# Gate and up biases in a grouped MoE feed-forward kernel: a two-row matmul in each block's accumulation in place of a spread copy added by VectorE

## The reference

```python
logits = y @ router_weight                                # 16 experts
topk_w, topk_i = top_k(logits, 2); topk_w = softmax(topk_w)
gu   = einsum('th,ehf->tef', y, gate_up_proj) + gate_up_proj_bias   # 256 columns: gate, up, gate, up ...
gate = minimum(gu[..., ::2], 7);  up = clip(gu[..., 1::2], -7, 7)
act  = (up + 1) * gate * sigmoid(1.702 * gate)
out  = einsum('tei,eih,te->th', act, down_proj, scores) + scores @ down_proj_bias
return x + out
```

## Time and profile before

| | us |
|---|---|
| median of 3 runs | 187.59 |
| lowest and highest | 185.32, 188.4 |
| span of the profiled execution | 185.1 |

### The profile page before, as it was taken

One profiled execution on the slowest core, in us unless ns is written; L12 is line 12 of the kernel. 1 busy time (PEld: TensorE's weight loads), 2 busy tenths in 40 slices (PEclk: granted clock), 3 DMA queues, 4 the chain that ended last, 5 costly groups with the idle time before them and its releaser, 6 DMA issues.

```text
span 185.1 us, 3421 instructions
## 1 busy us (share of the span) xinstructions
PE 135.2 (73%) x909; PEld 113.9 (62%) x910; DVE 115.6 (62%) x316; ACT 82.7 (45%) x172; POOL 90.6 (49%) x113
## 2 busy tenths in 40 slices
PE   6999999986193089999999999999999994000000
PEld 5749485836063056679899899899999983000000
DVE  0326878794893322244979878788788871006983
ACT  2224447474430942322566767676676764000000
POOL 6000487867878773000046675857667678710000
PEclk9999999998559755557999999999999999555555
DMA  4999723946829453610335365544665400029995
GB/s 129 281 343 348 224 84 76 344 145 197 311 80 268 168 178 134 170 58 4 103 102 162 117 206 148 158 147 144 197 184 185 145 30 28 0 63 359 355 384 200
DMA packets 30042, 32.21 MB, mean 174 GB/s; under 512 B 4954, under 2 KB 27982, under 8 KB 30032
## 3 DMA queue, kind: packets, MB, share of 16 engines
q1 hardware_dynamic: 24016, 21.57, 39.2%
q0 software_dynamic: 3840, 8.42, 13.0%
q10 hardware_dynamic: 2176, 2.10, 3.3%
HBM read 19.25 MB, written 14.84 MB: 184 GB/s over the span
## 4 chain that ended last, share of the span: by engine, by line
PE 66%; DVE 11%; issue 8%; DMA 7%; SPq 3%; POOL 2%; ACT 1%; POOLq 1%; DVEq 0%
PE bank L750 18%; PE bank L771 9%; PE bank L612 8%; PE bank L738 7%; DMA res<-pair_results 6%; PE bank L566 5%; PE bank L622 4%; PE bank L706 3%; PE bank L722 3%; PE bank L760 3%; PE bank L600 2%; SPq L365 2%; DVE topi L861 1%; POOL pair_results L448 1%; PE bank L587 1%
## 5 line engine op out<-in xcount | busy, mean ns | idle before, releaser
L448 POOL DMA_INDIRECT pair_results<-res,idx x48 | 48.2, 1004 | 43.3 <-ACT res L526 30.3
L420 POOL DMA_INDIRECT dispatched<-yrow,slot x32 | 36.5, 1141 | 26.3 <-DVE slot L881 17.4
L750 PE MATMUL bank<-wgu_hi,ygT_hi 128*128 x96 | 29.4, 306 | 0.0
L750 PE MATMUL bank<-wgu_raw,ygT_hi 128*128 x96 | 27.3, 284 | 0.0
L750 PE MATMUL bank<-wgu_hi,ygT_lo 128*128 x96 | 27.2, 283 | 0.0
L966 DVE TENSOR_TENSOR gub<-bank,gu_bias 128x256 f32<-128x256 f32 x48 | 18.1, 419 | 4.9 <-PE bank L750 4.6
L954 DVE TENSOR_TENSOR ygT_lo<-bank,ygT_hi 128x512 fp32r<-128x512 f32 x24 | 16.6, 691 | 7.0 <-ACT ygT_hi L509 5.9
L750 PEld LDWEIGHTS bank<-wgu_hi,ygT_hi 128*128 128x128 f32 x96 | 18.6, 194 | 0.3 <-issue 0.2
L750 PEld LDWEIGHTS bank<-wgu_raw,ygT_hi 128*128 128x128 f32 x96 | 18.7, 195 | 0.0
L750 PEld LDWEIGHTS bank<-wgu_hi,ygT_lo 128*128 128x128 f32 x96 | 18.6, 193 | 0.0
L771 PE MATMUL bank<-wd_hi,actT_hi 128*128 x48 | 15.6, 324 | 1.5 <-DVE actT_lo L959 1.5
(11 more groups left out here) (134 smaller groups left out, 262.8 us busy)
## 6 DMA issues: line engine op xcount, KB each, us to landing
yg<-dispatched SPq DMA_DIRECT2D x48, 128.5 KB, 2.5
wgu_raw<-in_L_ffn_gate_up_proj SPq DMA_DIRECT2D x8, 512.0 KB, 6.3
dispatched<-pad SPq DMA_DIRECT2D x4, 514.0 KB, 7.1
x_sb<-in_x SPq DMA_DIRECT2D x4, 512.0 KB, 4.9
wd_raw<-in_L_ffn_down_proj SPq DMA_DIRECT2D x8, 256.0 KB, 7.0
yrow<-pair_results SPq DMA_DIRECT2D x4, 512.0 KB, 7.2
out<-x_sb ACTq DMA_DIRECT2D x8, 256.0 KB, 5.0
yg<-pair_results SPq DMA_DIRECT2D x2, 512.0 KB, 6.2
```

The costliest lines, as they stand in the source:

```text
L420: nc.gpsimd.indirect_dma_start(out=xs, out_offset=bass.IndirectOffsetOnAxis(ap=slot[:, t, k:k + 1], axis=0), in_=yrow[:, t, :], in_offset= ...
L448: nc.gpsimd.indirect_dma_start(out=rs, out_offset=bass.IndirectOffsetOnAxis(ap=idx[:, s:s + 1], axis=0), in_=res[:, s, :], in_offset=None, ...
L750: last = nc.tensor.matmul(o, ygT[yp][:, u % 2, j, c, :], wgu[wp][:, bass.ds(e * (HC * F2) + c * F2, F2)], start=(c == 0 and n == 0), stop= ...
```

## The change

The biases are no longer spread over 128 partitions. The two parts (high and low) of all 16 bias rows are laid out as two long rows: SyncE writes `bsplit` to a DRAM buffer `gub_rows` (2 x 4096 values), and after the first choices of the second group are placed, waits for that and reads it back into `gub2`, now on 2 partitions. A constant `ones_r` of 2 x 128 ones is made by GpSimd. In the expert loop each block's accumulation now opens with a matmul of `ones_r` (2 rows, 128 columns) and the 256 bias columns of its expert, with `start=True`; the six matmuls of L750 add to it. So PSUM holds the biased result: ScalarE reads gate from PSUM when `s_gu` rises, and VectorE reads up from PSUM when ScalarE is done (`s_glu`). `add_bias` with its 48 instructions, `gub`, `gu_bias`, ScalarE's 8 copies, `spread_biases` with its 16 matmuls and its 12 spare transposes, and the selector `sel` go. Some counts of the constants' semaphore rise by one.

```diff
--- before.py
+++ after.py
...
@@ -55,6 +55,7 @@
     out_v = out.rearrange("b (t p) h -> p (b t) h", p=P)
     xs = nc.dram_tensor("dispatched", (XROWS, RW), FP32, kind="Internal").ap()
     rs = nc.dram_tensor("pair_results", (T * TOPK, H), FP32, kind="Internal").ap()
+    gub_rows = nc.dram_tensor("gate_up_bias_rows", (2, E * F2), FP32, kind="Internal").ap()
     rs_v = rs.rearrange("(k t p) h -> p k t h", p=P, k=TOPK)
 
     ctx = ExitStack()
@@ -79,11 +80,10 @@
         braw = sb("braw", [E, 2, F2])
         bsplit = {part: sb(f"bsplit_{part}", [E, 2, F2], FP32R) for part in PARTS}
 
-        gub2 = sb("gub2", [2 * E, F2], FP32R)
-        sel = sb("sel", [2 * E, E], FP32R)
+        gub2 = sb("gub2", [2, E * F2], FP32R)
+        ones_r = sb("ones_r", [2, P], FP32R)
 
         db3 = sb("db3", [3 * E, H], FP32R)
-        gu_bias = sb("gu_bias", [P, E * F2])
 
         ident = sb("ident", [P, P])
         tri = sb("tri", [P, P], BF16)
@@ -141,7 +141,6 @@
         idx = sb("idx", [P, RING], U32)
         ygT = {part: sb(f"ygT_{part}", [P, 2, 2, HC, P], FP32R) for part in PARTS}
         glu, up1, act = (room[:, n, :].rearrange("p (b j f) -> p b j f", b=2, j=2) for n in range(3))
-        gub = sb("gub", [P, 2, 2, F2])
         actT = {part: sb(f"actT_{part}", [P, 2, 2, P], FP32R) for part in PARTS}
         res = sb("res", [P, RING, H])
 
@@ -173,11 +172,8 @@
         s_bsplit = sem("s_bsplit")
         s_db3 = sem("s_db3")
         s_ups = sem("s_ups")
+        s_gub_rows = sem("s_gub_rows")
         s_gub2 = sem("s_gub2")
-        s_sel = sem("s_sel")
-        s_gu_bias_ps = sem("s_gu_bias_ps")
-        s_gu_bias = sem("s_gu_bias")
-        s_gub = sem("s_gub")
         s_wT_ps = sem("s_wT_ps")
         s_wT = sem("s_wT")
         s_side_ps = sem("s_side_ps")
@@ -328,9 +324,11 @@
                 sp.dma_start(db3[n * E:(n + 1) * E, :].bitcast(FP32),
                              bsplit[part][:, 1, :].bitcast(FP32)).then_inc(s_db3, 16)
             for n, part in enumerate(PARTS):
-                sp.dma_start(gub2[n * E:(n + 1) * E, :].bitcast(FP32),
-                             bsplit[part][:, 0, :].bitcast(FP32)).then_inc(s_gub2, 16)
+                sp.dma_start(gub_rows[n, :].rearrange("(e f) -> e f", e=E),
+                             bsplit[part][:, 0, :].bitcast(FP32)).then_inc(s_gub_rows, 16)
             first_choices_placed(sp, 1)
+            sp.wait_ge(s_gub_rows, 32)
+            sp.dma_start(gub2[:, :].bitcast(FP32), gub_rows).then_inc(s_gub2, 16)
             for e in range(5 * WE, 7 * WE, WE):
                 load_weights(e)
             first_choices_placed(sp, 2)
@@ -380,6 +378,7 @@
             nc.gpsimd.memset(ones_b[:, :], 1.0).then_inc(s_const, 1)
             nc.gpsimd.memset(ones_f[:, :], 1.0).then_inc(s_const, 1)
             nc.gpsimd.memset(ecol[:, :], 0.0).then_inc(s_const, 1)
+            nc.gpsimd.memset(ones_r[:, :].bitcast(FP32), 1.0).then_inc(s_const, 1)
             nc.gpsimd.iota(iota_e[:, :], pattern=[[1, E]], base=0, channel_multiplier=0,
                            allow_small_or_imprecise_dtypes=True).then_inc(s_const, 1)
             nc.gpsimd.iota(ebase[:, :], pattern=[[REGION, E]], base=P, channel_multiplier=0,
@@ -388,7 +387,7 @@
                            allow_small_or_imprecise_dtypes=True).then_inc(s_const, 1)
             nc.gpsimd.iota(iota_cnt[:, :], pattern=[[P, NT]], base=0, channel_multiplier=0,
                            allow_small_or_imprecise_dtypes=True).then_inc(s_const, 1)
-            pool.wait_ge(s_const, 9)
+            pool.wait_ge(s_const, 10)
 
             nc.gpsimd.affine_select(out=tri[:, :], in_=tri[:, :], compare_op=ALU.is_gt, fill=0.0,
                                     base=0, pattern=[[1, P]], channel_multiplier=-1).then_inc(s_const, 1)
...
@@ -498,11 +497,6 @@
                                      ACT.Copy).then_inc(s_scoreT, 1)
 
 
-            for n in range(E // 2):
-                act_e.wait_ge(s_gu_bias_ps, n + 1)
-                nc.scalar.activation(gu_bias[:, n * 2 * F2:(n + 1) * 2 * F2], bank[4 + n % 2][:, :],
-                                     ACT.Copy).then_inc(s_gu_bias, 1)
-
             def y_hi(p, u):
                 act_e.wait_ge(s_ygT_ps, p + 1)
                 need(act_e, s_gu, p - 1)
@@ -515,9 +509,9 @@
 
             def gelu_sigmoid(p, u):
 
-                act_e.wait_ge(s_gub, p + 1)
+                act_e.wait_ge(s_gu, p + 1)
                 need(act_e, s_act, p - 1)
-                nc.scalar.activation(glu[:, u % 2], gub[:, u % 2, :, 0:F2:2],
+                nc.scalar.activation(glu[:, u % 2], gu_ps[u % 2][:, :, 0:F2:2],
                                      ACT.Gelu_apprx_sigmoid).then_inc(s_glu, 1)
 
             def copy_res(i, u):
...
@@ -696,26 +690,10 @@
             pe.wait_ge(s_yn, 2 * NG)
             pe.wait_ge(s_scoreT, NG)
 
-            def spread_biases(n):
-
-                if n >= 2:
-                    pe.wait_ge(s_gu_bias, n - 1)
-                    warm_up(WARM_SPREAD, bank[4 + n % 2])
-                for j in range(2):
-                    e = 2 * n + j
-                    last = nc.tensor.matmul(bank[4 + n % 2][:, j * F2:(j + 1) * F2],
-                                            sel[:, e:e + 1].broadcast_to([2 * E, P]), gub2[:, :],
-                                            start=True, stop=True)
-                last.then_inc(s_gu_bias_ps, 1)
-
-
-            pe.wait_ge(s_gub2, 32)
-            pe.wait_ge(s_sel, 1)
+            pe.wait_ge(s_gub2, 16)
             pe.wait_ge(s_table, 1)
 
             for k in range(NT // 2):
-                for n in range(k * E // NT, (k + 1) * E // NT):
-                    spread_biases(n)
                 if k >= 6:
                     pe.wait_ge(s_db, k - 5)
                 for t in range(2 * k, 2 * k + 2):
@@ -745,12 +723,12 @@
                 for j in range(2):
                     e = owners[j]
                     o = gu_ps[u % 2][:, j, :]
+                    nc.tensor.matmul(o, ones_r[:, :], gub2[:, bass.ds(e * F2, F2)], start=True, stop=False)
                     for c in range(HC):
                         for n, (yp, wp) in enumerate(TERMS):
                             last = nc.tensor.matmul(o, ygT[yp][:, u % 2, j, c, :],
                                                     wgu[wp][:, bass.ds(e * (HC * F2) + c * F2, F2)],
-                                                    start=(c == 0 and n == 0),
-                                                    stop=(c == HC - 1 and n == len(TERMS) - 1))
+                                                    start=False, stop=(c == HC - 1 and n == len(TERMS) - 1))
                 last.then_inc(s_gu, 1)
 
             def transpose_act(i, u):
@@ -830,8 +808,6 @@
                 dve.wait_ge(s_bsplit, 1)
                 nc.vector.tensor_tensor(bsplit["lo"][:, :, :], braw[:, :, :], bsplit["hi"][:, :, :].bitcast(FP32),
                                         ALU.subtract).then_inc(s_bsplit, 1)
-                nc.vector.tensor_tensor(sel[:, :], ident[0:2 * E, 0:E], ident[0:2 * E, E:2 * E],
-                                        ALU.add).then_inc(s_sel, 1)
 
             def split_weights(experts):
                 for e in experts:
...
@@ -959,39 +935,28 @@
                 nc.vector.tensor_tensor(actT["lo"][:, u % 2], actT_ps[u % 2], actT["hi"][:, u % 2].bitcast(FP32),
                                         ALU.subtract).then_inc(s_alo, 1)
 
-            def add_bias(p, u, owners):
-
-                dve.wait_ge(s_gu, p + 1)
-                for j in range(2):
-                    last = nc.vector.tensor_tensor(gub[:, u % 2, j, :], gu_ps[u % 2][:, j, :],
-                                                   gu_bias[:, bass.ds(owners[j] * F2, F2)], ALU.add)
-                last.then_inc(s_gub, 1)
-
             def activate(p, u):
                 b = u % 2
-                dve.wait_ge(s_gub, p + 1)
-                nc.vector.tensor_scalar(up1[:, b], gub[:, b, :, 1:F2:2], 1.0 - LIMIT, 1.0 + LIMIT,
+
+                dve.wait_ge(s_glu, p + 1)
+                nc.vector.tensor_scalar(up1[:, b], gu_ps[b][:, :, 1:F2:2], 1.0 - LIMIT, 1.0 + LIMIT,
                                         ALU.max, ALU.min).then_inc(s_up1, 1)
                 dve.wait_ge(s_up1, p + 1)
-                dve.wait_ge(s_glu, p + 1)
                 need(dve, s_actT_ps, p - 1)
 
                 nc.vector.scalar_tensor_tensor(act[:, b], glu[:, b], GLU_MAX, up1[:, b],
                                                ALU.min, ALU.mult).then_inc(s_act, 1)
 
             def experts(i, first=False, last=False):
-                owners = table_values(mybir.EngineType.DVE, 1, i * RING, RING, E - 1)
                 for u in range(PAIRS_IN_BODY):
                     p = i * PAIRS_IN_BODY + u
                     if not (last and u == PAIRS_IN_BODY - 1):
                         y_lo(p + 1, u + 1)
-                    add_bias(p, u, owners[2 * u:2 * u + 2])
                     if not (first and u == 0):
```

(9 more changed lines are left out.)

## The result

The changed kernel takes 202.75 us (median of 6 runs, 201.23 to 207.38) against 188.0 for the kernel before (median of 6, 185.32 to 190.31). The ratio is 1.083, with a 95% interval of 1.078 to 1.089: it is slower. Every ratio in this document is taken over the runs within 1.5% of the fastest of the same kernel, and so isn't exactly that of the medians. The profiled execution's span is 199.8 us against 185.1, 14.7 more.

A forecast was written before the change was run, and what follows sets the result against it. TensorE was taken to bound the kernel. Start -3.8, bias matmuls +24.0, cold surplus +1.5, longer cold stretch +1.5 and end -2.2 sum to +21.0 us: profiled 185.1 becomes 206.1, and from the median 187.59 the forecast is 208.6, range 196 to 220.

The forecast's parts named there:

- the start: Ahead of the expert loop: loop starts at 77.1, held by the yg load, not 80.95; gain 3.8 us, bounds 3.5 and 4.1.
- The added read-back: On SyncE, behind the wait for group 1's scatter: counted as nothing, at most half a us of issue time.
- the price of a bias matmul: In the loop: emptying the array and unhidden weight loads make each cost 0.50 us, bounds 0.117 and 0.55.
- Rivals one, two and four: Loop: one, columns only, 188.6, chance 0.11; two, half of switching hidden, 198.2, 0.10; four, faster by over 2%, 0.03.
- the loop as a whole: Expert loop: 48 bias matmuls add 24.0 us, the cold ones' surplus 1.5, a longer half-clock stretch 1.5.
- the surplus of the cold bias matmuls: Loop start at half clock: the first five or so bias matmuls cost 0.29 us extra each, 1.5 us.
- a longer cold stretch: Loop start: half clock lasts 3 us longer, half of it lost, 1.5 us; bounds nothing and some 8 us.
- The price of a cold one: Loop start: a bias matmul at the half clock costs 0.79 us, 0.29 over the 0.50.
- rival three: Loop clock: stays at half speed for several pairs or throughout; five more make 223, all 24 about 270; chance 0.11.
- the end: After the loop: GpSimd has no scatter backlog, the last six taking 8.0 instead of 10.4; gain 2.2 us, bounds 0.6 and 2.5.

The follow-up runs named there:

- after_again: The changed kernel itself, nothing altered, profiled a second time: 203.14 us, span 201.4.
- twice: The changed kernel with each bias matmul issued twice, one straight behind the other, same result: 211.35 us (single run).
- rows96_act: The changed kernel with 96 rows under the bias matmul, all but two zero, cleared by ScalarE in idle time, bias rows loaded afterwards: 192.09 us (single run).
- no_bias: The changed kernel without its 48 bias matmuls, gate and up biases left out of the result: 183.42 us, ratio 0.984 to the kernel before.
- adjacent: The changed kernel with the two bias matmuls of a pair placed side by side, same result: 195.26 us (single run).
- dma_spread: The kernel before, VectorE additions kept, bias spread over 128 partitions by one DMA instead of matmuls, spare transposes and copies: 187.78 us, ratio 1.013.
- rows128: The changed kernel with 128 rows under the bias matmul, all but two zero, cleared by a GpSimd memset: 191.87 us, ratio 1.028 to the kernel before.

## Why the prediction was right, and where its sizes were off

The forecast was 208.6 us in 196 to 220, slower by over 2%, from a profile sum of +21.0. Measured: 202.75, and +14.7 in the spans.

**Right, with its size: the start.** The loop was to start at 77.1 and be held by the `yg` load; it started at 76.99, on the DMA. The gain is 3.9, forecast 3.8. The path is as forecast; that the number is met within 0.1 is partly luck. The same kernel started its loop at 78.6 in after_again, and the variants without a large memset started it between 75.9 (twice) and 82.5 (rows96_act). The added read-back cost nothing to see.

**Right, with its size: the price of a bias matmul.** Forecast 0.50, read off 16-row matmuls at the full clock and 32- and 48-row ones at the half; measured 0.50 in the middle of a pair, and a pair of 3.80 (forecast 3.75 to 3.8). That it lies in the change of rows, half before and half behind, and not in the instruction, is shown: half the changes, 3.42; the instructions doubled, 4.04, each one more costing 0.12; 128 rows, 3.03. Rivals one, two and four fall with that. The weight load is as short for 2 rows as for 128 (182 and 187 ns); what costs time is that it no longer runs beside a matmul, and the wait ahead of it. The Trainium skill's rule (TensorEngine Tiling, Key Properties), that changing the tiling mode drains TensorE, agrees with all of these; its tiling configurations of 32, 64 and 128 rows (same page, Available Configurations) agree with 64 rows paying and 96 not.

**Wrong in size: the loop as a whole.** The sum had +24.0 + 1.5 + 1.5 = +27.0 for the loop, measured +20.2. Two steps failed.

*The loop of before was read off one good pair.* The prediction took the pair from 95.28 to 98.06 as the loop ("the chain is TensorE alone") and let everything added be paid in full. But the loop's 70.1 us are 2.92 a pair: at the changes of body TensorE paused, and the first pairs were longer too (3.07, 2.96, 2.92 and 2.95 us). The changed kernel has none of this, and no_bias has the pauses again. The average pair goes from 2.92 to 3.76 (90.3 / 24), so 0.84 more and not 1.0; that is 20.2 in all. Of the missing part, 24 times 1.03 - 20.2 = 4.5 us, 1.1 go to the clock (below), and some 3.4 are left for the longer pairs of the kernel before, of which its chain shows 2.8 one by one (above).

*The cold stretch.* The terms for the surplus of the cold bias matmuls (1.5) and for a longer cold stretch (1.5) had the wrong sign in the profiled execution. From the table by stretches (columns as in the earlier trace rows):

```profile
76.99:79.79 2.80, 2.80 (x13) 2.47 (x13) 0.69 (x1) 0.60 (x1) 0.00 (x0) 0.50 0.81 235
79.79:85.77 5.98, 5.98 (x39) 4.86 (x39) 2.14 (x4) 2.06 (x6) 0.00 (x0) 1.00 0.13 28
```

Only 2.80 us of the loop, the transposes, ran cold, and 5.08 did before; half of the difference, 1.1 us, is a gain where I had charged 3.0, and outside the bounds I gave (nothing, and some 8 us). The step at fault is that bias matmuls would run cold at all: the clock rose at 79.79, just as the first one started, behind twelve transposes. The price of a cold one was right. In the kernel before, twelve cold gate/up matmuls took

```profile
83.70 2.58 PE bank L750 x12
```

which is 1.29 for six; in twice a change to the bias matmul and back took 0.51 + 1.58 - 1.29 = 0.80 at the half clock, worked out 0.79. When the clock rises stays open. In after_again it also rose 2.8 us into the loop, in no_bias 3.7 without any change of rows, in adjacent some 8 and in twice 14, though the same twelve transposes open all these loops, and in adjacent six 128-row matmuls more. So the long stretch of rival three exists; with the bias matmul as it was changed, neither of two profiles showed it.

**Right in kind, somewhat large: the end.** Forecast -2.2, measured -1.6. GpSimd does wait for ScalarE's results now, as the timeline shows:

```profile
168.57 0.60 ACT L520 ACTIVATE res<-bank 128x512 f32<-128x512 f32 x1
...
169.93 0.98 POOL L447 DMA_INDIRECT pair_results<-res,idx  x1 [1.09 <-ACT res L520]
...
176.38 0.99 POOL L447 DMA_INDIRECT pair_results<-res,idx  x1 [0.30 <-issue]
```

The last six run from 169.93 at 1.29 apart, as in the working. The result that the first of them needs is ready at 168.57 + 0.60 = 169.17, 1.6 behind the end of the last gate/up matmul (167.32 + 0.28), forecast 1.5. The term left out is the 0.8 from there to the scatter's start at 169.93: 176.38 - 167.6 = 8.8 and not 8.0, against 10.4 before, is 1.6 less.

## What to carry to other kernels

Count for a matmul of few rows not its columns but what stands beside it. Where TensorE is the bound, one matmul of 2 or 64 rows between full ones cost 0.50 us here, and filled up with zeros to 96 or 128 rows 0.12; where that can't be done, put the small ones side by side. Before charging an addition in full, divide the whole loop's time by its pairs: the difference to a clean pair is the slack that the addition takes up first; and don't count an earlier start of a loop as a sure gain: 2.8 us sooner was worth 0.7 of span in dma_spread, 3.1 sooner was kept in full in no_bias.

## What the runs showed of the hardware that was not expected

Between 64 and 96 rows the price of a bias matmul falls from 0.50 to 0.12 us. A GpSimd memset of 128 x 4096 values (3.50 us) went with a VectorE operation of 2.58 us that takes 0.41 without it, and ended 0.3 us after it; one case, not taken further. TensorE's speed at the same place differed between executions and kernels with the same instructions there: the eight 512-column matmuls of the first group took 3.63 us in the changed kernel, 5.68 in rows128 at a granted clock of 0.50, and 5.93 in rows96_act, where the profile gives the clock as 1.00. And a loop of which TensorE was never idle stayed at 0.50 for 2.8 us in the changed kernel and for 14 with doubled bias matmuls. The loop of rows96_act started 5.5 us later than that of the changed kernel, more than most of the effects under study, so only several runs of each kernel, or parts of a profile such as the pair, could tell kernels apart.
